# One up bias product per slot tile, three PSUM banks in turn, and a second stream that starts after twelve scans of the first

## The reference, cut to what matters

```python
x = x + mamba(layernorm(x))            # selective scan, 256 channels x 16 states
x = x + experts(layernorm(x))          # _L0_ffn_ref
x = x + linear_attention(layernorm(x))
x = x + experts(layernorm(x))          # the same weights again
...
def _ffn(x, wi, bi, wo, bo):
    return jax.nn.selu(x @ wi + bi) @ wo + bo
gate_logits = _ffn(xf, gate_wi, gate_bi, gate_wo, gate_bo)   # 128 logits
topv, topi = jax.lax.top_k(gate_logits, 2)
topv = topv / jnp.sum(topv, axis=-1, keepdims=True)
onehot = (topi[..., None] == jnp.arange(8)).astype(x.dtype)  # 8 experts
h = jax.nn.selu(jnp.einsum('nh,ehf->enf', xf, exp_wi) + exp_bi[:, None, :])
out_e = jnp.einsum('enf,efh->enh', h, exp_wo) + exp_bo[:, None, :]
```

## Time and profile before

| | before |
|---|---|
| median of 3 runs | 2962.91 us (2961.7 to 2963.11) |
| the profiled execution | 2957.25 us, of which the span of the core 2955.9 us |
| PE busy | 2287.9 us, 77% |
| DVE busy | 1866.6 us, 63% |
| ACT busy | 1356.9 us, 46% |
| POOL busy | 695.9 us, 24% |
| experts, both streams, first time | about 384 to 587 us |
| experts, both streams, second time | about 682 to 878 us |

### The profile page before, as it was taken

How to read it: one execution, slowest core, us unless ns; L and a number is a source line. 1 busy time by engine, 2 the same in 40 slices (tenths; PEclk the granted TensorE clock), 3 DMA queues, 4 the chain that set the end, 5 groups by cost and what they waited for, 6 DMA issues and landing times. The chain is left out here.

```text
span 2955.9 us, 40949 instructions
## 1 busy us (share of the span) xinstructions
PE 2287.9 (77%) x15598; PEld 1476.6 (50%) x15598; DVE 1866.6 (63%) x3594; ACT 1356.9 (46%) x2546; POOL 695.9 (24%) x610
## 2 busy tenths in 40 slices
PE   4777839574948887885888689766778989779889
PEld 1222439454934544453586368445455554555554
DVE  6989824493438978879898899753562242652331
ACT  4545304231427877873652464344334333435342
POOL 2727340404042212216591066000010100100000
PEclk9989969786969998996897699778789999899899
DMA  4000047304832111110000000202000000000000
GB/s 175 0 0 1 1 134 234 99 1 152 241 93 87 43 33 40 40 33 5 0 1 1 0 1 1 70 1 68 13 1 1 1 2 1 8 1 1 1 1 7
DMA packets 70708, 117.80 MB, mean 40 GB/s; under 512 B 9616, under 2 KB 46224, under 8 KB 70160
## 3 DMA queue, kind: packets, MB, share of 16 engines
q1 hardware_dynamic: 64112, 104.69, 12.0%
q0 software_dynamic: 4096, 8.40, 0.9%
q10 hardware_dynamic: 2304, 2.10, 0.3%
HBM read 84.61 MB, written 16.78 MB: 34 GB/s over the span
## 5 line engine op out<-in xcount | busy, mean ns | idle before, releaser
L185 DVE SCALAR_TENSOR_TENSOR conv<-conv_in,held_l1a,conv 128x512 f32<-128x512 f32 x288 | 244.2, 871 | 29.4 <-ACT conv L166 26.4
L179 POOL TENSOR_TENSOR long<-long,product 128x512 f32<-128x512 f32 x136 | 214.1, 1593 | 198.9 <-ACT product L166 190.4
L209 POOL MEMSET wide_q<- 128x1536 f32 x8 | 11.0, 1379 | 887.1 <-DVE stream_b L182 837.3
L179 POOL TENSOR_TENSOR part<-state,c_rows 128x512 f32<-128x512 f32 x128 | 161.1, 1285 | 72.1 <-issue 53.0
L179 POOL TENSOR_TENSOR qk<-conv,held_const 128x512 f32<-128x512 f32 x64 | 92.3, 1443 | 349.4 <-DVE conv L185 349.4
L182 DVE TENSOR_SCALAR grown<-grown 128x512 f32<-128x512 f32 x92 | 39.6, 430 | 210.6 <-ACT grown L166 163.7
L148 PE MATMUL ps<-part,held_const 128*128 128x512 f32 x256 | 147.1, 659 | 13.3 <-POOL part L179 8.4
L191 DVE TENSOR_TENSOR_SCAN state<-decay,ps 128x512 f32<-128x512 f32 x128 | 146.9, 1193 | 0.0
L188 DVE TENSOR_REDUCE wide_q<-ps 128x4 f32<-128x512 f32 (+1 forms) x128 | 113.5, 950 | 49.8 <-PE ps L148 49.8
L166 ACT ACTIVATE probs<-ps 128x768 f32<-128x768 f32 x128 | 96.5, 808 | 88.2 <-PE ps L148 88.0
L148 PE MATMUL ps<-yn,nT 128*128 128x192 f32 (+2 forms) x640 | 115.6, 313 | 20.3 <-DVE yn L179 17.6
(11 more groups left out here) (503 smaller groups left out, 6135.2 us busy)
## 6 DMA issues: line engine op xcount, KB each, us to landing
ring_a<-in_experts SPq DMA_DIRECT2D x46, 512.0 KB
ring_b<-in_experts SPq DMA_DIRECT2D x46, 512.0 KB
turned<-conv SPq DMA_DIRECT2D x256, 64.0 KB
ring<-lags SPq DMA_DIRECT2D x64, 128.0 KB
held_l3f<-in_l3f SPq DMA_DIRECT2D x1, 2824.0 KB
xg<-rows_x_a SPq DMA_DIRECT2D x10, 256.0 KB
xg<-rows_x_b SPq DMA_DIRECT2D x10, 256.0 KB, 5.2
rows_y_a<-y SPq DMA_DIRECT2D x10, 256.0 KB, 5.4
```

The costliest lines, as they stand in the source:

```text
L179: return self.vector(self.real.tensor_tensor(out, a, b, op), columns(out), out, a, b)
L185: return self.vector(self.real.scalar_tensor_tensor(out, a, p, b, first, second), columns(out) + 60, out, a, b)
L209: return self.vector(self.real.memset(out, value), columns(out) // 2, out)
```

## The change

The expert biases are laid out with one row per expert and chunk (32 rows, three parts of bfloat16 each). The row of the picked expert is selected once per tile by DVE into `lifted`, and one product with 512 moving columns adds the bias to the whole bank, where four products with 128 columns did. The transposes and the up products take three banks (0, 1, 2) in turn, and the down product takes bank 3. PE issues up(j + 2) ahead of down(j). The weight ring has four buffers, and the x tiles a ring of three slices that is refilled in the loop. The second stream's first DVE instruction waits for twelve `state` signals of the first stream's first mamba, that is 6 of its 16 steps with two scans each. The planner's costs for issuing DMAs are raised.

```diff
-        self.engine.free += 1.0      # scatter, gather
+        self.engine.free += 1.27
...
-        self.engine.free += 0.3      # value
+        self.engine.free += 0.7
...
-        self.engine.free += 0.1      # dma_start
+        self.engine.free += 0.35
...
-W_RING = 3
+W_RING = 4
+X_RING = 3
 CHUNK = 4
-X_GROUP = [0, 0, 1, 1, 1, 1]
+STARTS = range(CHUNK, SLOT_TILES, CHUNK)
...
+    uses = [("turn", 0), ("up", 0), ("up", 1)]
+    for j in range(SLOT_TILES):
+        uses += [("up", j + 2)] * (j + 2 < SLOT_TILES) + [("turn", (j + 3) // CHUNK)] * (j + 3 in STARTS)
+    bank_turn, bank_up = ({k: at % 3 for at, (what, k) in enumerate(uses) if what == name} for name in ("turn", "up"))
+    freed = {use: (s.kept_x, k + 1) if what == "turn" else (s.hidden, GATE + k + 1)
+             for use, (what, k) in zip(uses[3:], uses)}
...
             for c in range(FC):
-                out = tile(st.ps(j % 2), c)
-                pe.matmul(out, tile(W, c), tile(b.xgT[:, j // CHUNK % 2, :], j % CHUNK), start=True, stop=False)
-                mm = pe.matmul(out, tile(m.bias16[0:SPLIT, :], c), pick(j), start=False, stop=True)
-            mm.then_inc(s.up)
+                pe.matmul(tile(out, c), tile(W, c), tile(b.xgT[:, j // CHUNK % 2, :], j % CHUNK), start=(c == 0),
+                          stop=False, skip_group_check=True)
+            pe.matmul(out.rearrange("p (c n) -> p c n", c=FC), b.lifted[0:SPLIT, j, :],
+                      m.chunk16[0:SPLIT, :].unsqueeze(2).to_broadcast([SPLIT, FC, P]), start=False, stop=True,
+                      skip_group_check=True).then_inc(s.up)
...
         yield from up(0)
+        yield from up(1)
         for j in range(SLOT_TILES):
-            if j % CHUNK == 1 and j // CHUNK + 1 < len(SLICES):
-                yield from turn(j // CHUNK + 1)
-            if j + 1 < SLOT_TILES:
-                yield from up(j + 1)
+            if j + 2 < SLOT_TILES:
+                yield from up(j + 2)
+            yield pe.wait_ge(s.hidden, GATE + j + 1)
+            if j + 3 in STARTS:
+                yield from turn((j + 3) // CHUNK)
             yield from down(j)
...
+            ve.tensor_tensor(b.lifted[0:SPLIT, :, :], m.bias_up[0:SPLIT, :].unsqueeze(1).to_broadcast([SPLIT, SLOT_TILES, P]),
+                             b.picked[0:SPLIT, :].unsqueeze(2).to_broadcast([SPLIT, SLOT_TILES, P]), ALU.mult
+                             ).then_inc(s.picked)
...
+        for q in range(X_RING):
+            load_x(q)
         for j in range(SLOT_TILES):
...
+            if j == at and q + X_RING < len(SLICES):
+                yield sp.wait_ge(s.turn, q + 1)
+                load_x(q + X_RING)
...
+    B.begin = (layers["a"][0].s.state, 12)
     layers["a"].append(state_space(m, A, keep.x))
```

More of the change, by code:

```diff
@@ L722, in experts @@
         R.w_count[j % W_RING] += 1
+    x_before = list(R.x_count)
+    for q in range(len(SLICES)):
+        R.x_count[q % X_RING] += 1
     w_at = lambda j: 16 * (w_before[j % W_RING] + j // W_RING + 1)
@@ L738, in experts @@
                of_tile=[P, SLOT_TILES, E], expert=[P, SLOT_TILES], rows=([1, SLOT_TILES], I32),
-               picked=([P, SLOT_TILES], BF16), slot=[P, CHOICES], miss=[P, CHOICES], slots=([P, CHOICES], U32))
+               picked=([P, SLOT_TILES], BF16), lifted=([P, SLOT_TILES, P], BF16), slot=[P, CHOICES], miss=[P, CHOICES], slots=([P, CHOICES], U32))
     first, then = Arena(m, a.at, 4 * TT * P), Arena(m, a.at, 4 * TT * P)
@@ L743, in experts @@
     first, then = Arena(m, first.end, a.end - first.end), Arena(m, first.end, a.end - first.end)
-    xg = first.place([P, SLOT_TILES, P], name="xg")
+    xg = first.place([P, X_RING * CHUNK, P], name="xg")
     back = then.place([P, CHOICES, P], name="back")
@@ L787, in turn @@
             at, n = SLICES[q]
-            yield pe.wait_ge(R.x_loaded[X_GROUP[q]], 16 * X_GROUP.count(X_GROUP[q]) * (done + 1))
-            if q:
-                yield pe.wait_ge(s.kept_x, q)
+            yield pe.wait_ge(R.x_loaded[q % X_RING], 16 * (x_before[q % X_RING] + q // X_RING + 1))
+            if q == 0:
+                yield pe.wait_ge(s.slots, 1)
             else:
-                yield pe.wait_ge(s.logits, len(every))
+                yield pe.wait_ge(*freed["turn", q])
             for i in range(n):
-                mm = pe.transpose(st.tiles(3)[:, i, :], xg[:, at + i, :], m.ident)
+                mm = pe.transpose(st.tiles(bank_turn[q])[:, i, :], xg[:, q % X_RING * CHUNK + i, :], m.ident)
             mm.then_inc(s.turn)
@@ L814, in down @@
             hidden = b.hidden[:, j % FC, :]
-            yield pe.wait_ge(s.hidden, GATE + j + 1)
             if j:
@@ L863, in scalar @@
         yield from grow(GATE, w.ln_alpha)
+        yield from grow(GATE + 1, w.ln_alpha)
         for j in range(SLOT_TILES):
[L865 to L868, removed]
+            if j + 2 < SLOT_TILES and j + 2 not in STARTS:
+                yield from grow(GATE + j + 2, w.ln_alpha)
+            if j + 3 in STARTS:
+                yield from keep_x((j + 3) // CHUNK)
+            if j + 2 in STARTS:
+                yield from grow(GATE + j + 2, w.ln_alpha)
             yield from keep_y(j)
@@ L2935, in build @@
     held["ffn"], held["route"] = m.hold(low, "ffn"), m.hold(low, "route")
-    m.bias16 = low.place([P, (FC + 1) * P], BF16, name="bias16")
+    bias16 = low.many(up=([P, P], BF16), down=([P, P], BF16), chunk=([P, FC], BF16))
+    m.bias_up, m.bias_down, m.chunk16 = bias16.up, bias16.down, bias16.chunk
     rings = low.at
@@ L2939, in build @@
     split = Arena(m, rings, low.at - rings)
-    m.bias_rest, m.bias_mid = split.place([P, (FC + 1) * P], name="rest"), split.place([P, (FC + 1) * P], BF16, name="mid")
+    held["biases"] = m.hold(split, "biases")
+    m.bias_rest, m.bias_mid = split.place([P, P], name="rest"), split.place([P, P], BF16, name="mid")
     late = Arena(m, block, 64 << 10)
@@ L3030, in first_loads @@
     def first_loads(sp):
-        order = ("const", "masks", "l0a", "rows", "ffn", "route", "l0b", "l1a", "l1f", "l1b")
+        order = ("const", "masks", "l0a", "rows", "ffn", "route", "biases", "l0b", "l1a", "l1f", "l1b")
         for group in order:
```

76 lines of the change are left out of this document (42 added, 34 removed).

## The result

The changed kernel takes 3007.55 us (median of 4, 2999.6 to 3008.81); the kernel before, run beside it, 2963.01 (2961.7 to 2964.69). The ratio is 1.0146, 95% interval 1.013 to 1.0162: 1.5% slower, where 2.2% faster was forecast. The profiled execution has a span of 3006.7 us against 2955.9.

The account below looks back on a forecast made before the run. It took DVE to bound the mamba layers at 91%, with holes in both experts layers where the streams do the same work. Stream b's steps gave -73 + 16 - 9 = -66 us from 2957, plus 5.7 for the median: 2897 us, range 2820 to 2965.

Parts of the forecast that it names:

- b's second gather near 785 us: End of stream b's second experts loop: its gather was to begin near 785 us in place of 851.
- slots to loop: Stream b, each experts layer: 20.3 us of scatter plus 8 for the x tiles; 48 us before in the second.
- the start itself: First mamba layer: a's first scan near 52 us, b's first statistics near 75, all of b 57 us later.
- the bias product: Experts loop on PE: one 512-column up bias product saves 0.16 us per tile, 15 us if PE bounds every tile.
- The queue order: Stream b's x tiles no longer wait behind stream a's on SP; second slots to loop 20 us shorter than 48.
- slots at 415: Stream b's first routing: DVE at 91% ends at 395, plus 20 for b's gate alone; before, 404.79 with POOL free.
- gather to the next slots -20: Stream b between the experts layers: 118 us before, 20 less because b is alone or nearly so on DVE.
- a lone loop at 4.18: Experts loops of b: 4.18 us per tile at weight-load speed, 101 us per loop, 21 and 20 us less.
- a 90 us ahead of b: Stream a some 90 us ahead where it was 30, so less work is shared later: 0 to 35 us, 9 taken.
- The stop beside POOL's phases: Scatters and gathers now fall on the other stream's work and make its engines wait: 16 us added.
- The first: Rival: late start lost and not won back, loops of 122 and 121 us as before; 2980 us, chance 0.13.
- The third, the clock: Rival: a lone loop leaves PE idle, its clock falls, about 5 us per tile; about 2930 us, chance 0.2.

Follow-up runs that it names:

- e13: The changed kernel with stream b waiting until stream a has finished its second experts layer, so a runs alone till then; 3374.18 us, one execution.
- e3: The changed kernel without the late start and with the planner's old prices, so the new loop alone; 2922.61 us, ratio 0.9968 to the kernel before.
- e17: The same kernel as e3, run again on another chip; 2949.73 us, ratio 0.9947 to the kernel before.
- e2: The kernel before with only the late start of twelve state steps added; 2971.83 us, ratio 1.0129 to the kernel before.
- e7: The kernel before with a late start of four state steps; ratio 0.999 to the kernel before.
- e8: The kernel before with a late start of 32 state steps, all of stream a's first mamba layer; ratio 1.0029 to the kernel before.
- e15: The kernel before with a late start of 20 state steps; ratio 1.0144 to the kernel before.
- e9: The kernel before with its 128 indirect DMAs replaced by plain ones of the same size and queue; 2886.11 us, ratio 0.9731 to the kernel before.
- e10: The changed kernel with its indirect DMAs replaced by plain ones of the same size and queue; 2932.22 us, ratio 0.9889 to the kernel before.
- e16: The new loop with the planner's old prices and a late start of four state steps; ratio 0.9974 to the kernel before.
- e1: The changed kernel with stream b's late start taken out, all else kept; 2943.23 us, ratio 1.0038 to the kernel before.

## Why the prediction was wrong, step by step

The forecast had b's second gather near 785 us; it is at 882.7, 98 us late, and that is most of the 111 by which the median was missed. (The 785 already has the 9 us in it that were to be won behind the gather; by the terms ahead of it the sum is 794.) By the forecast's own steps, a loop from its first up product to its gather:

| step of stream b | before | forecast | change | alone (e13) |
|---|---|---|---|---|
| slots | 404.8 (POOL free) | 415 | 440.2 | |
| slots to loop | 36.9 | 28 | 41.2 | 27.4 |
| first loop | 122 | 101 | 109.2 | 87.0 |
| gather to next slots | 118 | 98 | 137.9 | 108.7 |
| slots to loop | 48 | 28 | 38.9 | 26.6 |
| second loop | 121 | 101 | 115.3 | 83.4 |

Every row was missed in the same direction, by 25, 13, 8, 40, 11 and 14 us.

**Right:** the start itself (a's first scan at 47.4, forecast 52, and b's first statistics at 70.41, forecast 75) and the bias product. Between 480 and 538 us 26 tiles pass PE, 2.23 us each with their transposes, in e3 36 tiles in 80 us, 2.22, where the kernel before had 33 in 80, 2.42: 0.2 us less, forecast 0.16. The new loop as a whole, with `lifted` and the rings, is worth 9 us in e3 and 14 in e17 (by the medians). The queue order was half right: from b's second slots to its loop 48 us became 39 and not 28, and the same step of the first layer grew from 37 to 41. With the start alone both take 27 us in e2, but 34 to 40 in e7, e8 and e15; what decides between these was not tested.

**The first failed step: slots at 415.** It assumed DVE at 91% with the same instructions, and stream a routed near 320. Stream a did end its mamba 22 us earlier, but its slots came at 386.9 us, 3 us later than before. The last residual addition of a's mamba and a's slots, in the kernel before and in the change:

```profile
330.83 0.69 DVE L179 TENSOR_TENSOR x<-x,ps 128x512 f32<-128x512 f32 x1 [1.76 <-PE ps L148]
...
383.62 0.16 DVE L179 TENSOR_TENSOR slots<-slot,miss 128x16 uint32<-128x16 f32 x1
```

```profile
309.00 0.69 DVE L179 TENSOR_TENSOR x<-x,ps 128x512 f32<-128x512 f32 x1 [1.11 <-PE ps L148]
...
386.89 0.17 DVE L179 TENSOR_TENSOR slots<-slot,miss 128x16 uint32<-128x16 f32 x1
```

So a's gate and routing took 77 us beside b's mamba, where they took 52 beside b's gate and take 39 alone (e13), and the whole lead was lost there. With 4, 12 and 20 steps in the kernel before (e7, e2, e15) a's slots stay within some 5 us of their place too; only the 32 steps of e8 bring them forward, to 351.7. Of the 25 us more, 15 lie in the chain from `onehot` to `slots`: it took 22 us (364.93 to 386.89), where it took 7.3 before and takes 7.6 alone. The planner put b's products and scans, some 11 us of them, between its small instructions, and some of those ran longer beside POOL's:

```profile
369.91 0.39 DVE L191 TENSOR_TENSOR_SCAN running<-held_route,ps 128x128 f32<-128x128 f32 x1
370.33 1.25 DVE L179 TENSOR_TENSOR used<-running,held_route 128x64 f32<-128x64 f32 x1
371.51 1.28 DVE L179 TENSOR_TENSOR ps<-dx,ps 128x512 f32<-128x512 f32 x2
372.70 0.21 DVE L188 TENSOR_REDUCE tiles<-used 128x8 f32<-128x64 f32 x1
372.83 0.27 DVE L179 TENSOR_TENSOR running<-running,ps 128x128 f32<-128x128 f32 x1
373.03 2.32 DVE L191 TENSOR_TENSOR_SCAN state<-decay,ps 128x512 f32<-128x512 f32 x2
375.27 0.39 DVE L191 TENSOR_TENSOR_SCAN ends<-ones,tiles 128x8 f32<-128x8 f32 x1
375.58 0.27 DVE L179 TENSOR_TENSOR running<-running,ps 128x128 f32<-128x128 f32 x1
375.77 1.29 DVE L179 TENSOR_TENSOR of_tile<-held_route,ends 128x184 f32<-128x184 f32 x1
```

To b's slots DVE was idle some 23 us more (15 of it forecast, at the start) and busy 31 us more: 6.4 for two `lifted`, 5.5 for a's first tiles, most of the rest because the same instructions run longer. Those sums are over the instructions up to b's first slots in both traces (385.9 and 440.4 us); two groups, before and after:

```profile
L185 DVE SCALAR_TENSOR_TENSOR xs<-conv_in,held_l0a,xs 128x512 f32<-128x512 f32 x24 | 18.0, 751 | 1.0
L179 DVE TENSOR_TENSOR dx<-dx,gate 128x512 f32<-128x512 f32 x8 | 5.9, 737 | 0.1
```

```profile
L185 DVE SCALAR_TENSOR_TENSOR xs<-conv_in,held_l0a,xs 128x512 f32<-128x512 f32 x24 | 20.6, 857 | 1.2 <-DVE xs L185 0.5
L179 DVE TENSOR_TENSOR dx<-dx,gate 128x512 f32<-128x512 f32 x8 | 7.7, 964 | 0.1
```

**The second, and the largest: "gather to the next slots -20".** It took a lone stream to be fast there; alone it needs 108.7 and not 98, and in the change b is not alone: a's scatter and loop lie beside b's gate, and it takes 137.9, 40 us more than forecast. The distance isn't needed for most of it, though: in e3 and e17, with the new loop and no late start, the same step takes 130 and 132 us, and in e2, with the start alone, 131. What stretches it in each was not tested.

**The third: "a lone loop at 4.18".** Alone a loop is even shorter, 83 to 87 us, 3.6 to 3.8 a tile (the 3.2 us of a load that the forecast set beside its 4.18 was for DMAs of a software path, while SP issues these loads). But a lag of 50 us is less than a loop, so b's loop is never alone for long: PE is full in 476 to 540 and 759 to 818 us, a's gather then takes half of PE's time, and the loops have 109 and 115 us. The forecast used the lone price where the distance did not give a lone loop. Nor was a 90 us ahead of b, as the forecast had it, but 65 (the second gathers, 817.9 and 882.7). The stop beside POOL's phases was put at 16 us for four; PE is idle for some 10 us in each 20 us phase (9.75 of 20 busy), but as e9 and e10 show the kernel before pays as much.

**The rivals.** The first came nearest (the start is lost and not won back), with its point of decision: b's gather after 592 us. It came at 590.6 and the loss was there all the same, 3007.6 against its 2980; it had loops of 122 and 121 us, which were 109 and 115, and left out the +20 between gather and slots. The third, the clock: in lone loops it is 0.91 and 0.94 (e13), so what the rival said of them does not hold. The low clocks are in the POOL phases (0.51 to 0.77) and between the layers (0.75 in 611 to 671 us). The start alone cost 1.3% in e2 at a mean clock of 0.886, with 0.887 for the kernel before on that chip, so a lower mean clock isn't needed for that part.

**The chance of a term left out.** No step of the forecast allowed that a stage not touched changes by its order. Here the piece behind b's combine gave +12 (1074 to 1086) of the 51 in the first pair of traces and +3 in the second, not clearly more than two traces of one kernel differ by; in the other kernels it was between -31 (e16) and +27 (e1, another chip) from the 1074 of the kernel before. The planner's prices, in the diff and left out of the sum, cost 0.7% by themselves in the kernel before. Why exactly the clock falls in these orders was not settled.

## What to carry to other kernels

No late start tried here paid: 4 to 32 steps gave ratios of 0.999 to 1.014 with the old loop, and 0.997 to 1.010 with the new one, which alone has 0.995 to 0.997. Before two streams are set apart, price each stage with the other stream's actual neighbour beside it, not alone, and follow the stream that is to get ahead as well: here its lead went into its own gate. In a kernel whose order comes from a planner every edit is also a new order; run each part by itself, and don't take a gain below some 0.5% for the edit's own before it has been seen under a second order.

## What the runs showed of the hardware

- While 16 indirect DMAs are issued on POOL (20 us), PE works 0 to 10 of 20 us in the kernel before and 9 to 13 in the change; beside a loop it is 9 to 10 in both. ACT took one product 9.6 us after its end, idle for 7.8 of them. With plain DMAs from the same queue (0.54 us each) PE works 6.65 of 9 beside a loop.
- `lifted`, 96 x 2944 bfloat16 with both operands repeated by stride, takes 3222 ns, 1.09 ns a column. The forecast had 4 us at most for one and took 6 for the two of stream b, which are 6.4. The Trainium skill, VectorE: DVE Perf Modes, section "What auto-detection actually checks", gives the double rate only if every tensor is 16-bit with step 1 or -1; `picked` is read with step 0, and the trace agrees with the single rate: float32 products of 128 and 512 columns take 0.29 and 0.68 us here, 1.0 ns a column more.
- Small DVE instructions with two SBUF inputs took four to six times as long beside a POOL instruction: `used` 1.25 us against 0.20, `of_tile` 1.29 against 0.34. POOL's at that time, two instructions of 1.25 us in each row:

```profile
369.01 2.50 POOL L179 TENSOR_TENSOR part<-state,c_rows 128x512 f32<-128x512 f32 x2 [2.92 <-PE ps L148]
374.37 2.49 POOL L179 TENSOR_TENSOR part<-state,c_rows 128x512 f32<-128x512 f32 x2 [2.86 <-issue]
```

  `used` ended at 371.6 and `of_tile` at 377.1, each 0.1 to 0.2 us behind the POOL instruction beside it (371.5, 376.9). The addition with an input in PSUM that stands beside the same POOL instruction (375.58) keeps its 0.27 us. The Trainium skill, GPSIMD Engine Reference, section "1. Specifications", says that GpSimd's SBUF interfaces are shared with VectorE, with contention for DVE instructions that have two SBUF inputs; the rows agree.
- In the first lone loop of e13 the granted clock is 0.91 with PE busy 62 of 88 us.
- One kernel in one order, traced on two chips (e3, e17): the same time up to b's first slots (394.4 and 394.3 us), and from there to b's second gather, which is where the experts layers lie, 419 and 454 us.
